# Attention 1's values and softmax sums in 32-column tiles, its padding mask by row tiles, and the segment sums in 512-column matmuls

## The chip, the cores and the metric

One NeuronCore of one Trainium2 chip runs the whole program. The metric is the device time of one execution in microseconds, the median of several runs.

## The reference

A decoder stack of four layers runs over 32 sequences of 128 tokens with 256 channels, and a context of the same shape. All arithmetic is float32.

```python
x = L0(x, ctx, Wq, Wk, Wv)          # plain attention, 16 heads; the kernel computes it for one sequence only, then adds it
# L1: Mamba-2 block, then cross attention with 8 heads of 32 channels
zxbcdt = rms(x) @ in_proj_w;  conv over 4 taps, silu
h = h * exp(dt*A) + (dt*xh) * B;  y = h . C             # a scan over the tokens, 8 heads
x = x + rms((y + D*xh) * silu(z)) @ out_proj_w
q, k, v = ln(x) @ Wq, ctx @ Wk, ctx @ Wv
scores = where(pad_mask, -1e9, q k^T / sqrt(32))
x = x + (softmax(scores) @ v) @ Wo
# L2: causal self attention and cross attention, 16 heads of 16, each + layernorm, then a small FFN + layernorm
# L3: causal cross attention, 16 heads, + layernorm, FFN with gelu
```

## The kernel before

The kernel is written engine by engine. Each sequence is a lane; four lanes (G = 4) make an iteration, and eight iterations are written out without loops. The work of a lane is cut into some 80 tasks (K1, quads1, turn1_0, values1, finish1, Wo, x2T and so on). A table of due times, `TASKS`, says when in a lane's life each task comes, in units of which 56 make an iteration and 14 the distance of one lane from the next. `in_order` sorts all tasks of the lanes in flight by due time, and every engine issues its part of each task in that one order. So in the steady part each engine's order repeats with every lane, and the order of tasks within it is that of their due times modulo 14. The first and the last iteration, in which the pipeline fills and drains, have tables of their own (`FIRST_BODY`, `LAST_BODY`). Engines run freely otherwise; semaphores make them wait.

The four attentions of a lane (a_ = 1 to 4) are units of the same steps. `quads` (L521 to L535) are the scores on TensorE: 32-row tiles side by side, each into its own bank of `score`, over a mask laid first where there is one (L521 with `ident_bf` as the full 128-row stationary operand and the padding row moving for attention 1, L526 for the causal ones). `scores` is the softmax's shift on VectorE (L1029 row maximum, L1030 subtraction, 1024 columns each) and the exponential on ScalarE (L832). `turn` transposes the exponentials on TensorE (L479, eight transposes in two halves) and ScalarE copies them to `weights` (L837). `values` are the matmuls with the values into the one bank `output`. Attention 1 has one part, the others two (`turn3_0`, `turn3_1`).

For attentions 2 to 4, `values` keeps the value block stationary in tiles of 32 columns (L572), so that channels come out on partitions; ScalarE copies `output` to `attT` (L843), TensorE turns it back (`back`), VectorE divides by the sum, which is one more column of the values (L1042, L1043, `weighted`). For attention 1, `values1` keeps the exponentials stationary (128x128) and moves the 33 columns of each head's values with a column of ones (L563), so that tokens come out on partitions. `finish1` on VectorE divides straight from `output`, `oT` turns the result on TensorE, ScalarE copies it to `actT`, and `Wo` projects it. Each use of `output` waits until the earlier user has read it (`output_read`). All other results of TensorE go through three banks, `ring`, taken in turn in the order of the tasks (`RING_JOBS`).

The Mamba block sums the log decays over segments of the sequence with triangular matrices of ones: `log_decays` on GpSimd (L1315) writes `after` times a rate into `decay`, and TensorE multiplies each of the eight heads' blocks with `before` (L641, in the task pairs).

In the trace a float32 matmul stands as two records, a bf16 matmul and a transpose as one.

Of the kernel before, what the change touches and what calls it, by code (L numbers as in the profile page):

```python
# [9 lines left out]
ALU = mybir.AluOpType  # L10
# [7 lines left out]
G = 4  # L18
# [33 lines left out]
    loadx=0.97, loadc=7.03, x1=1.35, x1r=2.07, xhat=2.42, xhatT=2.83, dt=3.57, softplus=5.74, am=7.96, xbc=3.22,  # L52
# [9 lines left out]
    finish3=37.48, norm3=37.6, x4T=37.59, fc1=38.37, fc2=38.9, norm4=39.09, K4=35.59, V4=43.75, x5T=39.37, Q4=39.68,  # L62
    xhatT=0.1, unit3=31.59, finish1=18.05, norm5=46.16, x6T=46.75, up=48.43, finish4=45.87, V3=34.69, xnT=14.02,
    proj=11.76, decayed=10.17, down=63.56, V2=23.46, softplus=5.04, am=7.89, K1=11.47, silu=8.25, pairs=9.54,
    store=74.57, quads=-0.51, K3=29.22, unit1=14.91, uT=11.66, n2=25.73, xhat=-2.92, unit4=40.55, loadc=30.78,
    dt=4.05, xbc=0.22, z=4.26, conv=7.05, Y=11.3, K2=20.29, x3T=28.9, Q2=19.77, attT=2.47, row=28.72, Q3=30.23,
    V1=9.91, Q1=14.22, x2T=19.45, loadx=-18.17, x1=-6.65, x1r=-3.34, values=3.3, norm2=28.83, oT=18.78, Wo=19.09,
    e2=21.9, unit2=21.27, n3=35.21, finish2=28.23, back=3.58, e3=35.09, turn=1.64)
LAST_BODY = dict(
    back=2.17, Q1=18.14, Q3=28.27, softplus=20.82, pairs=24.7, finish3=33.84, norm3=35.82, x4T=36.58, fc1=36.86,  # L70
    fc2=38.11, norm4=38.72, K4=37.39, V4=43.04, x5T=38.53, Q4=38.9, unit4=40.07, finish4=44.5, decayed=17.41,
    Y=-81.98, uT=31.74, proj=9.65, x1r=-32.33, values=2.12, finish2=25.14, norm2=26.85, x3T=26.95, row=27.68,
    K3=29.28, V3=26.95, e3=30.67, n3=33.63, unit3=30.43, V1=-2.63, xnT=6.1, unit1=14.68, xhatT=24.83, am=-18.19,
    down=61.44, xbc=12.12, x6T=48.84, up=52.2, Q2=19.83, V2=24.61, unit2=21.43, attT=1.73, store=41.77, turn=1.34,
    loadx=20.76, x1=-9.01, x2T=19.36, loadc=14.65, dt=-15, xhat=-2.71, z=31.47, K1=-43.07, conv=27.2, silu=-20.42,
    norm5=47.08, e2=22.59, n2=24.73, finish1=18.03, oT=17.98, Wo=18.87, K2=20.87, quads=-0.45)
# [150 lines left out]
WITHIN = """dt xnT; xbc xnT; z xnT; Q1 oT; Wo x2T; K2 x3T; Q2 x3T; V2 x3T; Q3 x4T; fc1 x5T; Q4 x6T; pairs decayed; e2 Q3; e3 Q4;  # L227
# [1202 lines left out]
```

## Time and profile before

| | |
|---|---|
| median of 3 runs | 1966.96 us (1964.62 to 1967.33) |
| the profiled execution's own time | 1966.0 us |
| its span, first to last instruction | 1964.2 us |
| TensorE matmuls, weight loads | 91%, 80% of the span |
| VectorE, ScalarE, GpSimd | 76%, 63%, 27% |
| DMA engines | busy in the first 20 us, then about 10 GB/s |
| mean granted TensorE clock | 0.97 of full speed |

The busy shares are for the whole span; the pipeline fills for some 200 us and drains for some 100. The chain of work that ended last lies on TensorE for 63% of the span and on VectorE for 28%, ScalarE has 4%.

### The profile page before, as it was taken

To read this page: it belongs to the slowest core of one execution; us is meant where nothing else is said; L and a number is where in the kernel's file an instruction comes from. 1 tells how busy PE (TensorE), PEld (TensorE's weight loads), DVE (VectorE), ACT (ScalarE), POOL (GpSimd) and SP (SyncE) were. 2 spreads that over 40 slices of the span, in tenths; PEclk is the share of its full clock that TensorE was granted. 3 is DMA by queue.
4 is the path that set the end of the run, shared out by engine and by line. 5 is a ranking of instruction groups with operands and counts; after the bars stand their busy time and mean duration, and the time that the engine had idled before them with its cause. 6 is when DMAs were issued, how large, how long until landed. Compare 5 with 4: busy or idle time off the path is not lost.

```text
span 1964.2 us, 47829 instructions
## 1 busy us (share of the span) xinstructions
PE 1796.8 (91%) x18704; PEld 1566.6 (80%) x18704; DVE 1502.0 (76%) x3163; ACT 1236.3 (63%) x2668; POOL 525.2 (27%) x1288
## 2 busy tenths in 40 slices
PE   4678899999999999999999999999999999999876
PEld 3567788888888888888888888888888888888765
DVE  3367788877888888888888888888888888788652
ACT  2245567666667766666677666667666666677443
POOL 1221323322333232223333322333232123323110
PEclk7699999999999999999999999999999999999888
DMA  6000000000000000000000000000000000000000
GB/s 231 12 4 4 2 15 4 10 10 10 10 7 10 4 10 10 10 10 10 7 4 10 10 10 10 10 7 10 5 10 10 10 10 10 7 4 4 4 4 6
DMA packets 26141, 26.46 MB, mean 13 GB/s; under 512 B 2240, under 2 KB 25024, under 8 KB 25792
## 3 DMA queue, kind: packets, MB, share of 16 engines
q1 hardware_dynamic: 25920, 23.41, 3.6%
q8 instruction: 152, 2.49, 0.5%
q14 instruction: 69, 0.57, 0.1%
HBM read 19.21 MB, written 4.19 MB: 12 GB/s over the span
## 4 chain that ended last, share of the span: by engine, by line
PE 63%; DVE 28%; issue 4%; ACT 4%; POOL 1%; DMA 0%; DVEq 0%; SPq 0%; ACTq 0%; POOLq 0%
PE ring L491 18%; PE ring L485 17%; PE ring L479 14%; DVE neg_max L1029 8%; DVE shifted L1030 7%; PE score L535 6%; PE output L563 3%; PE ring L649 3%; ACT shifted L832 2%; DVE conv L1121 1%; DVE res L1017 1%; PE score L526 1%; DVE att L1015 1%; DVE dx L1141 1%; DVE dbx L1139 1%
## 5 line engine op out<-in xcount | busy, mean ns | idle before, releaser
L1270 POOL TENSOR_TENSOR stat<-stat 128x1 f32<-128x1 f32 x224 | 125.8, 561 | 969.5 <-DVE stat L1000 961.6
L1029 DVE TENSOR_REDUCE neg_max<-score 128x8 f32<-128x1024 f32 x226 | 276.2, 1222 | 108.5 <-PE score L535 101.9
L832 ACT ACTIVATE shifted<-shifted 128x1024 f32<-128x1024 f32 x226 | 240.8, 1065 | 112.4 <-DVE shifted L1030 112.1
L1030 DVE TENSOR_TENSOR shifted<-score,neg_max 128x1024 f32<-128x1024 f32 x226 | 276.6, 1224 | 7.8
L837 ACT COPY weights<-ring 128x512 f32<-128x512 f32 x452 | 243.8, 589 | 49.3 <-PE ring L479 43.2
L479 PE MATMUL ring<-const,shifted 128*128 128x128 f32 x1808 | 249.3, 282 | 22.2 <-ACT shifted L832 19.6
L479 PEld LDWEIGHTS ring<-const,shifted 128*128 128x128 f32 x1808 | 205.2, 145 | 47.1 <-ACT shifted L832 33.4
L1113 DVE SCALAR_TENSOR_TENSOR conv<-raw,vectors,conv 128x128 f32<-128x128 f32 x576 | 184.3, 375 | 5.7
L485 PE MATMUL ring<-actT,w_q 128*128 128x128 f32 x1024 | 139.8, 281 | 4.3 <-ACT actT L809 4.3
L535 PE MATMUL score<-K,QB 32*128 32x128 f32 x3616 | 137.1, 285 | 0.3 <-ACT K L809 0.2
L485 PEld LDWEIGHTS ring<-actT,w_q 128*128 128x128 f32 x1024 | 129.9, 196 | 8.2 <-ACT actT L809 6.5
L535 PEld LDWEIGHTS score<-K,QB 32*128 32x128 f32 x3616 | 112.5, 186 | 27.3 <-issue 27.3
L809 ACT COPY actT<-ring 128x256 f32<-128x256 f32 x256 | 96.2, 377 | 53.1 <-PE ring L479 50.5
L843 ACT COPY attT<-output 128x512 f32<-128x512 f32 x97 | 56.3, 580 | 114.1 <-PE output L572 113.9
L485 PE MATMUL ring<-actT,w_up 128*128 128x128 f32 x1024 | 119.7, 275 | 0.5 <-ACT actT L809 0.5
L879 ACT ACTIVATE conv<-ring,vectors 128x128 f32<-128x128 f32 x192 | 74.6, 467 | 71.8 <-PE ring L485 71.7
L491 PE MATMUL ring<-w_down,gT 128*128 128x256 f32 x512 | 116.8, 381 | 1.3 <-issue 1.3
L485 PEld LDWEIGHTS ring<-actT,w_up 128*128 128x128 f32 x1024 | 117.2, 192 | 0.9 <-ACT actT L809 0.7
L485 PE MATMUL ring<-cT,w_k 128*128 128x128 f32 x768 | 109.9, 287 | 0.4 <-ACT raw L881 0.4
L491 PEld LDWEIGHTS ring<-w_down,gT 128*128 128x128 f32 x512 | 97.8, 192 | 14.7 <-issue 1.4
L572 PE MATMUL output<-weights,V 128*32 128x128 f32 x3104 | 105.9, 277 | 2.5 <-ACT weights L837 2.5
L491 PE MATMUL ring<-w_v,cT 128*128 128x256 f32 x384 | 101.3, 387 | 0.0
(162 smaller groups left out, 3721.6 us busy)
## 6 DMA issues: line engine op xcount, KB each, us to landing
cT<-in_ctxT SPq DMA_DIRECT2D x32, 128.0 KB, 2.1
x_in<-in_x SPq DMA_DIRECT2D x32, 128.0 KB, 2.2
out<-result SPq DMA_DIRECT2D x32, 128.0 KB, 1.7
row_all<-in_rows SPq DMA_DIRECT2D x1, 1420.0 KB, 10.4
w_in<-in_in_proj SPq DMA_DIRECT2D x1, 1288.0 KB, 7.8
w_q<-in_q SPq DMA_DIRECT2D x4, 256.0 KB, 8.3
w_k<-in_k SPq DMA_DIRECT2D x4, 256.0 KB, 6.2
w_v<-in_v SPq DMA_DIRECT2D x4, 256.0 KB, 6.7
```

What stands on the lines that cost most here:

```text
L479: last = nc.tensor.transpose(t[:, c * P:(c + 1) * P], src[:, c * P:(c + 1) * P], ident)
L485: last = mm(t[:, at:at + P], w[:, c, cols:cols + P], xT[:, c, :], start=(c == 0), stop=(c == n - 1))
L491: last = mm(t[:, at:at + hi - lo], xT[:, c, :], w[:, c, lo:hi], start=(c == 0), stop=(c == n - 1))
L535: last = mm(score[:, r, at:at + P], QB[rows_of, l, c, e, :], keys[rows_of, l, c, :], start=(not masked and at == 0), stop=(at + P == width))
L572: last = mm(output[ROWS_OF[r], four * P:(four + 1) * P], V2[:, l, h, :], exps_of(t, heads_of(a_, t).index(h)), start=True, stop=True)
L809: nc.scalar.copy(dst.rearrange("p c k -> p (c k)"), t[:, 0:n]).then_inc(read, 1)
L832: run(e, e, ACT.Exp, scale=SCALE8 if a_ == 1 else 0.25).then_inc(S["exps"], 1)
L837: nc.scalar.copy(weights[:, buffer(it, a_, l, t, WEIGHT_BUFFERS), half * 4 * P:(half + 1) * 4 * P], t_[:, :]).then_inc(read, 1)
L1029: step(nc.vector.tensor_reduce(m, s, AX_X, ALU.max, negate=True))
L1030: tt(shifted[:, n, :].rearrange("p (b h k) -> p b h k", b=shape[1], k=P), s, m.unsqueeze(3).broadcast_to(shape), ALU.add).then_inc(S["shif ...
L1113: last = stt(conv[:, l % 2, c, :], raw[:, l % 2, c, k:k + P], conv_w[:, c, k:k + 1], conv[:, l % 2, c, :], ALU.mult, ALU.add)
L1270: tt(stat[:, l, 10:11], stat[:, l, 2:3], stat[:, l, 4:5], ALU.pow).then_inc(S[done], 1)
```

## The change

- `values1`: instead of 8 matmuls with the exponentials stationary there are 16 in tiles of 32 columns with the exponentials moving: 8 with a block of ones (`ones`, 128x32) write each head's sum, repeated over its 32 channels, into the upper 256 columns of `output`, and 8 with the head's values write the products into the lower 256. `V1` has no column of ones any more.
- `finish1` on VectorE: a reciprocal of 128x256 from `output` into `rec1`, and a product of 128x256 straight into `actT`. It waits on four semaphores (one for each row tile) instead of one. The helper `weighted` serves attentions 0 and 2 to 4 alone.
- The task `oT` (two transposes, a ring job, ScalarE's copy) is gone, and `Wo` waits for `finish1`.
- `quads1`: the padding mask is laid with 32 rows of ones as the stationary operand for each row tile, the mask divided by 32.
- `pairs`: the segment sums are two matmuls with `after` stationary and 512 columns moving, instead of eight with 128; GpSimd prepares `before` times the rate instead of `after`.
- All due times differ, in the three tables.

Its core (the other due times, declarations and lists of tasks are left out):

```diff
 TASKS = dict(
...
-    z=4.31, K1=12.37, V1=13.56, conv=7.15, silu=7.78, pairs=8.82, decayed=9.65, Y=9.99, uT=10.61, proj=11.58,
-    xnT=13.12, Q1=13.77, finish1=18.09, oT=18.47, Wo=19.52, x2T=20.56, K2=20.9, Q2=20.87, V2=22.59, e2=21.84,
-    n2=25.32, finish2=27.24, norm2=28.11, x3T=29.12, row=29.4, K3=29.67, Q3=29.4, V3=32.63, e3=30.41, n3=31.69,
...
-    finish4=45.34, norm5=47.45, x6T=47.68, up=48.91, down=52.32, store=65.56, unit1=15.41, unit2=21.73, unit3=31.28,
-    unit4=39.91, quads=-0.32, scores=0, turn=1.39, values=2.22, attT=1.91, back=3.09)
...
+    z=4.22, K1=12.67, V1=14.56, conv=7.48, silu=8.18, pairs=8.71, decayed=9.11, Y=9.97, uT=10.7, proj=11.76,
+    xnT=12.98, Q1=13.57, finish1=19.59, Wo=19.69, x2T=19.74, K2=21.24, Q2=21.09, V2=22.68, e2=21.9, n2=23,
+    finish2=27.5, norm2=28.48, x3T=29.28, row=29.34, K3=29.79, Q3=29.34, V3=32.81, e3=30.68, n3=31.9, finish3=36.61,
...
+    norm5=47.41, x6T=47.95, up=49.36, down=52.34, store=56.37, unit1=15.37, unit2=21.85, unit3=31.65, unit4=39.88,
+    quads=-0.09, scores=0, turn=1.43, values=2.54, attT=1.85, back=2.97)
...
@@ -351,7 +347,9 @@
         keep = sb("keep", [P, G, H16])
         neg_max = sb("neg_max", [P, 2, HEADS])
         K1 = sb("K1", [P, G, DC, P])
-        V1 = sb("V1", [P, G, H8, DH8 + 1])
+        V1 = sb("V1", [P, G, H8, DH8])
+        ones = sb("ones", [P, DH8])
+        rec1 = sb("rec1", [P, D])
         V2 = sb("V2", [P, G, H16, P // TILES])
 
         decay = sb("decay", [P, 2, MH, P])
@@ -518,7 +516,9 @@
                     for r, rows_of in enumerate(ROWS_OF):
                         free(r)
                         if a_ == 1:
-                            mm(score[:, r, 0:width], ident_bf[:, :], padding_bf[:, :].unsqueeze(1).broadcast_to((P, DC, P)),
+
+                            mm(score[:, r, 0:width], ones_bf[rows_of, :],
+                               padding_bf[rows_of, :].unsqueeze(1).broadcast_to((P // TILES, DC, P)),
                                start=True, stop=False)
                             continue
@@ -559,10 +559,15 @@
 
                 evacuated_all(it, *V_job, *[j for t in range(PARTS[a_]) for j in turn_jobs(a_, l, t)])
                 if a_ == 1:
-                    for i, h in enumerate(heads_of(1, 0)):
-                        last = mm(output[:, h * (DH8 + 1):(h + 1) * (DH8 + 1)], exps_of(0, i), V1[:, l, h, :],
-                                  start=True, stop=True)
-                    last.then_inc(S["output_full"], 1)
+
+                    for at, summed in ((D, True), (0, False)):
+                        for c in range(DC):
+                            for r in range(TILES):
+                                h = TILES * c + r
+                                last = mm(output[ROWS_OF[r], at + c * P:at + (c + 1) * P], ones[:, :] if summed else V1[:, l, h, :],
+                                          exps_of(0, heads_of(1, 0).index(h)), start=True, stop=True)
+                                if not summed and c == DC - 1:
+                                    last.then_inc(S[f"att_full{r}"], 1)
                     return
 
                 for four in range(H16 // TILES):
@@ -637,9 +642,8 @@
                 pe.wait_ge(S["am"], nth(it, l))
                 for half in range(2):
                     t, full = claim(it, f"ld{half}", l)
-                    for i in range(4):
-                        last = mm(t[:, i * P:(i + 1) * P], decay[:, m, 4 * half + i, :], before, start=(i == 0), stop=(i == 3))
-                    last.then_inc(full, 1)
+                    mm(t[:, :], after, decay[:, m, 4 * half:4 * half + 4, :].rearrange("p h k -> p (h k)"),
+                       start=True, stop=True).then_inc(full, 1)
 
             def Y(it, l):
                 t, full = claim(it, "Y", l)
@@ -668,12 +672,8 @@
                 evacuated(it, "xnT", l, ("Q1", l))
                 project_T(it, "Q1", l, square["q1"], actT[:, l])
 
-            def oT(it, l):
+            def Wo(it, l):
                 pe.wait_ge(S["output_read"], nth_output(it, 1, l))
-                flip(it, "oT", l, att[:, l, :], DC)
-
-            def Wo(it, l):
-                evacuated(it, "oT", l, ("Wo", l))
                 project(it, "Wo", l, square["o1"], actT[:, l])
 
             def x2T(it, l):
@@ -1032,20 +1032,12 @@
 
             def weighted(it, a_, l, step, dst):
 
-                heads, dh = (H8, DH8) if a_ == 1 else (H16, DH16)
-                if a_ == 1:
-                    dve.wait_ge(S["output_full"], nth(it, l))
-                    o, read = output[:, 0:heads * (dh + 1)].rearrange("p (h e) -> p h e", h=heads), S["output_read"]
-                else:
-                    t, read = filled(it, *back_job(a_, l))
-                    o = t[:, :].rearrange("p (h e) -> p h e", h=heads)
-                step(nc.vector.reciprocal(rec[:, l, 0:heads], o[:, :, dh]))
-                tt(dst.rearrange("p (h e) -> p h e", h=heads), o[:, :, 0:dh],
-                   rec[:, l, 0:heads].unsqueeze(2).broadcast_to((P, heads, dh)), ALU.mult).then_inc(read, 1)
-                if a_ == 1:
-                    dve.wait_ge(S["output_read"], nth_output(it, a_, l))
-                else:
-                    evacuated(it, *back_job(a_, l))
+                t, read = filled(it, *back_job(a_, l))
+                o = t[:, :].rearrange("p (h e) -> p h e", h=H16)
+                step(nc.vector.reciprocal(rec[:, l, :], o[:, :, DH16]))
+                tt(dst.rearrange("p (h e) -> p h e", h=H16), o[:, :, 0:DH16],
+                   rec[:, l, :].unsqueeze(2).broadcast_to((P, H16, DH16)), ALU.mult).then_inc(read, 1)
+                evacuated(it, *back_job(a_, l))
 
             def x1(it, l):
@@ -1078,7 +1070,7 @@
             dve.wait_ge(S["rates"], 1)
             ts(decay_rate, decay_rate, -1.0, None, ALU.mult).then_inc(S["ready_in"], 1)
             ts(keep_row[:, :], pad_u8[:, :], -1.0, 1.0, ALU.mult, ALU.add)
-            ts(padding_bf[:, :], pad_u8[:, :], MASKED, None, ALU.mult)
+            ts(padding_bf[:, :], pad_u8[:, :], MASKED / (P // TILES), None, ALU.mult)
             ts(skip, skip, 0.5, None, ALU.mult)
             dve.wait_ge(S["later_in"], 16)
             ts(causal_bf[:, :, :], dx[:, 0, :].rearrange("p (q k) -> p q k", q=TILES), MASKED, None, ALU.mult)
@@ -1167,6 +1159,14 @@
                     evacuated(it, "proj", l)
                     moments(l, step, S["seed3"])
 
+                def finish1(l):
+
+                    for r in range(TILES):
+                        dve.wait_ge(S[f"att_full{r}"], nth_output(it, 1, l))
+                    step(nc.vector.reciprocal(rec1[:, :], output[:, D:]))
+                    tt(actT[:, l, :, :].rearrange("p c k -> p (c k)"), output[:, 0:D], rec1[:, :],
+                       ALU.mult).then_inc(S["output_read"], 1)
+
                 def Wo(l):
                     t, read = filled(it, "Wo", l)
                     tt(res[:, l, :], t[:, 0:D], res[:, l, :], ALU.add).then_inc(read, 1)
@@ -1261,7 +1261,7 @@
 
             nc.gpsimd.memset(V2[:, :, :, DH16 + 1:], 0.0).then_inc(S["ones_col"], 1)
             nc.gpsimd.memset(V2[:, 0, :, DH16:DH16 + 1], 1.0).then_inc(S["ones_col"], 1)
-            nc.gpsimd.memset(V1[:, :, :, DH8], 1.0).then_inc(S["ones_col"], 1)
+            nc.gpsimd.memset(ones[:, :], 1.0).then_inc(S["ones_col"], 1)
             nc.gpsimd.memset(raw[:, :, :, 0:TAPS - 1], 0.0).then_inc(S["pads_zero"], 1)
 
             def root(it, l, seed, done):
@@ -1312,7 +1312,7 @@
 
                     wait_for(S["dt"], nth(it, l))
                     step(tt(dts[:, 5, l, :], dts[:, 10, l, :], decay_rate, ALU.mult))
-                    tt(decay[:, l % 2, :, :], after.unsqueeze(1).broadcast_to((P, MH, P)),
+                    tt(decay[:, l % 2, :, :], before.unsqueeze(1).broadcast_to((P, MH, P)),
                        dts[:, 5, l, :].unsqueeze(2).broadcast_to((P, MH, P)), ALU.mult).then_inc(S["am"], 1)
 
                 def first_query(a_, l):
```

## Rows read from the trace of the kernel before

**Rows 1.** Stretches of the span: busy us of each engine, granted clock, DMA.
```profile
1000.00:1250.00 250.00, 239.48 (x2548) 209.61 (x2547) 208.47 (x440) 172.06 (x372) 77.44 (x191) 1.00 0.03 8
...
1850.00:1900.00 50.00, 39.31 (x350) 34.19 (x351) 26.18 (x53) 25.25 (x50) 5.06 (x11) 0.76 0.00 1
```

**Rows 2.** Waits of TensorE, 250 to 1750 us: total, times, longest.
```profile
PE ring L479 <- DVE att L1010: 19.9, 26, 1.1
PE ring L491 <- DVE nonzero L1180: 18.5, 26, 0.7
```

**Rows 3.** Timeline of TensorE in one period: start, us, group, records; idle in brackets.
```profile
1019.15 1.95 PE L641 MATMUL ring<-const,decay 128*128 128x128 f32 x16
...
1043.20 0.84 PE L521 MATMUL score<-padding_bf,ident_bf 128*128 128x256 bf16 x4
...
1047.76 1.08 PE L572 MATMUL output<-weights,V 128*32 128x128 f32 x32
1048.77 0.61 PE L702 MATMUL ring<-q_first,K 128*128 128x8 f32 x4
1049.45 1.09 PE L479 MATMUL ring<-const,shifted 128*128 128x128 f32 x8
1050.38 0.38 PE L479 MATMUL ring<-const,att 128*128 128x128 f32 x2
1050.69 1.17 PE L535 MATMUL score<-K,QB 32*128 32x128 f32 x32
...
1054.97 1.87 PE L563 MATMUL output<-V,weights 128*128 128x33 f32 x16
1056.68 0.17 PE L708 MATMUL ring<-nonzero,ones_bf 128*128 128x16 bf16 x1
...
1058.54 0.38 PE L479 MATMUL ring<-const,att 128*128 128x128 f32 x2
1058.76 1.03 PE L491 MATMUL ring<-w_v,cT 128*128 128x256 f32 x4
...
1062.40 1.04 PE L479 MATMUL ring<-const,shifted 128*128 128x128 f32 x8
...
1068.73 0.43 PE L526 MATMUL score<-causal_bf,ident_bf 32*32 32x512 bf16 x16
```

**Rows 4.** Timeline of ScalarE in the same period.
```profile
1060.27 1.07 ACT L837 COPY weights<-ring 128x512 f32<-128x512 f32 x2
1061.23 1.07 ACT L832 ACTIVATE shifted<-shifted 128x1024 f32<-128x1024 f32 x1
```

**Rows 5.** Timeline of VectorE in the same period.
```profile
1051.98 1.23 DVE L1029 TENSOR_REDUCE neg_max<-score 128x8 f32<-128x1024 f32 x1 [2.13 <-PE score L535]
...
1054.38 0.24 DVE L1042 RECIPROCAL rec<-ring 128x16 f32<-128x16 f32 x1
...
1056.26 0.15 DVE L1000 TENSOR_SCALAR stat<-stat 128x1 f32<-128x1 f32 x1
...
1057.30 0.42 DVE L1043 TENSOR_TENSOR att<-output,rec 128x256 f32<-128x256 f32 x1
1057.76 1.22 DVE L1029 TENSOR_REDUCE neg_max<-score 128x8 f32<-128x1024 f32 x1
1059.01 1.22 DVE L1030 TENSOR_TENSOR shifted<-score,neg_max 128x1024 f32<-128x1024 f32 x1
...
1070.38 1.22 DVE L1029 TENSOR_REDUCE neg_max<-score 128x8 f32<-128x1024 f32 x1
```

**Rows 6.** Groups by shape, whole span: count, busy us, mean ns of one, idle.
```profile
L1042 DVE RECIPROCAL rec<-ring 128x16 f32<-128x16 f32 x97 | 24.1, 248 | 27.3 <-PE ring L479 27.3
...
L1180 DVE TENSOR_SCALAR nonzero<-ring 128x16 bf16<-128x16 f32 x64 | 10.9, 170 | 23.4 <-PE ring L702 23.4
...
L1042 DVE RECIPROCAL rec<-output 128x8 f32<-128x8 f32 x32 | 6.3, 197 | 7.3 <-PE output L563 7.3
```

**Rows 7.** Line L1017 from 1000 to 1060 us: shortest, median, longest ns.
```profile
L1017 DVE SCALAR_TENSOR_TENSOR res<-att,stat,row_all x4: 484/484/873, 1003.9 to 1044.0; 128x256 f32<-128x256 f32 x4
```

More of the change, by code:

```diff
@@ L60 @@
+    finish2=27.5, norm2=28.48, x3T=29.28, row=29.34, K3=29.79, Q3=29.34, V3=32.81, e3=30.68, n3=31.9, finish3=36.61,
+    norm3=36.75, x4T=37.23, fc1=37.52, fc2=37.98, norm4=38.07, K4=36.21, V4=42.63, x5T=39.16, Q4=39.7, finish4=45.19,
+    norm5=47.41, x6T=47.95, up=49.36, down=52.34, store=56.37, unit1=15.37, unit2=21.85, unit3=31.65, unit4=39.88,
+    quads=-0.09, scores=0, turn=1.43, values=2.54, attT=1.85, back=2.97)
 FILL = (0, 14, 28, 42)
 FIRST_BODY = dict(
-    finish3=37.48, norm3=37.6, x4T=37.59, fc1=38.37, fc2=38.9, norm4=39.09, K4=35.59, V4=43.75, x5T=39.37, Q4=39.68,
@@ L63 @@
[L63 to L67, printed above, removed]
@@ L68 @@
-    e2=21.9, unit2=21.27, n3=35.21, finish2=28.23, back=3.58, e3=35.09, turn=1.64)
-LAST_BODY = dict(
[L70 to L76, printed above, removed]
+    finish3=37.33, norm3=37.37, x4T=37.59, fc1=38.04, fc2=38.55, norm4=38.92, K4=39.1, V4=43.64, x5T=39.66, Q4=39.76,
@@ new lines @@
+    xhatT=0.09, unit3=31.85, finish1=18.11, norm5=48.14, x6T=47.84, up=50.88, finish4=46.84, V3=29.86, xnT=13.05,
+    proj=11.85, decayed=10.08, down=55.89, V2=23.44, softplus=5.49, am=9.22, K1=10.91, silu=8.17, pairs=9.36,
+    store=64.14, quads=-0.41, K3=29.49, unit1=15.24, uT=11.74, n2=25.81, xhat=-0.73, unit4=41.13, loadc=33.21,
+    dt=4.25, xbc=0.34, z=4.68, conv=6.9, Y=10.24, K2=20.61, x3T=28.86, Q2=19.99, attT=2.17, row=28.82, Q3=29.22,
+    V1=7.64, Q1=14.3, x2T=19.54, loadx=-9.52, x1=-6.71, x1r=-4.39, values=2.86, norm2=28.24, Wo=19.53, e2=24.49,
@@ new lines @@
+    unit2=21.74, n3=35.42, finish2=27.88, back=3.18, e3=35.13, turn=1.78)
+LAST_BODY = dict(
+    back=1.89, Q1=19.84, Q3=29.94, softplus=32.92, pairs=-6.12, finish3=34.13, norm3=35.1, x4T=35.57, fc1=35.69,
+    fc2=36.29, norm4=37.67, K4=34.51, V4=42.78, x5T=37.53, Q4=39, unit4=40.14, finish4=44.43, decayed=14.75, Y=-71.03,
+    uT=36.09, proj=2.93, x1r=-37.16, values=1.79, finish2=26.91, norm2=28.44, x3T=29.06, row=29.64, K3=29.8, V3=34.07,
+    e3=31.51, n3=31.85, unit3=31.19, V1=-21.76, xnT=6.27, unit1=15.62, xhatT=15.25, am=-32.45, down=63.46, xbc=6.87,
+    x6T=50.06, up=53.42, Q2=21.31, V2=24.9, unit2=22.06, attT=1.75, store=34.27, turn=0.95, loadx=21.42, x1=-27.29,
+    x2T=20.17, loadc=7.04, dt=2.63, xhat=-3.03, z=20.5, K1=-29.46, conv=30.86, silu=-8.65, norm5=46.13, e2=21.99,
+    n2=24.53, finish1=17.64, Wo=19.8, K2=21.4, quads=-0.57)
@@ L223, in wait @@
         eng.wait_ge(semaphore, value)
-WITHIN = """dt xnT; xbc xnT; z xnT; Q1 oT; Wo x2T; K2 x3T; Q2 x3T; V2 x3T; Q3 x4T; fc1 x5T; Q4 x6T; pairs decayed; e2 Q3; e3 Q4;
+WITHIN = """dt xnT; xbc xnT; z xnT; xnT Q1 finish1 Wo x2T; K2 x3T; Q2 x3T; V2 x3T; Q3 x4T; fc1 x5T; Q4 x6T; pairs decayed; e2 Q3; e3 Q4;
 quads1 Q2; quads2 Q3; quads3 Q4; e2 K3 e3 K4; quads2 K3; quads3 K4; values2 V3; values3 V4; n2 e3; values2 n3; finish2 norm2;
@@ L775, in _ @@
             do = dict(K1=K_1, V1=V_1, xhatT=xhatT, xbc=xbc, z=z, pairs=pairs, Y=Y, uT=flip_u, proj=proj, xnT=xnT,
-                      Q1=Q1, oT=oT, Wo=Wo, x2T=x2T, Q2=Q2, K2=K_2, V2=V_2, x3T=x3T, row=row, Q3=Q3, K3=K3, V3=V3, x4T=x4T,
+                      Q1=Q1, Wo=Wo, x2T=x2T, Q2=Q2, K2=K_2, V2=V_2, x3T=x3T, row=row, Q3=Q3, K3=K3, V3=V3, x4T=x4T,
                       fc1=fc1, fc2=fc2, K4=K4, V4=V4,
```

13 lines of the change are left out of this document (5 added, 8 removed).

## The prediction

> **What bounds the kernel now.** I read the stretches of the span first. From about 250 to 1750 us the picture repeats: in 250 us TensorE is busy for 239.5 us at a granted clock of 1.00 (its 2.4 GHz level), VectorE for 208.5 us, and only the last hundred microseconds thin out [rows 1]. The kernel is a software pipeline with a period of one lane (one sequence). The waits of TensorE in the steady part are few and recurring: 26 waits for L1010 and 26 for L1180 in 1500 us, so the period is about 57 us, and in each TensorE stands about 0.7 us at either [rows 2]. The timeline gives the period more sharply, 56.7 us. By busy share TensorE (96%) is the bound, VectorE (83%) is not. That is too coarse, for the two hand over to each other: the softmax of a unit is two VectorE passes of 1.2 us each (L1029, L1030), then ScalarE's exponential (L832), then TensorE's transposes. So I went through one period of both engines' timelines and asked for each wait who was late. Four handovers repeat:
>
> (a) from the scores of attention 4 until the transposes of attention 1 (1049.45), VectorE works without a gap and TensorE follows it;
> (b) from there to 1062.40, the second transposes of attention 3, TensorE is the slower. VectorE waits 2.13 us for the scores of quads3, and the exponential at 1061.23 starts only when ScalarE has emptied the transposes of the first half, two copies L837 from 1060.27, though its input was ready at 1060.23 (the shift, 1059.01 + 1.22) [rows 3 to 5];
> (c) from 1062.40 until the scores of quads2 TensorE alone; VectorE reaches them at 1070.38, just as they end [rows 3, 5];
> (d) then VectorE again until x4T, and TensorE from x4T to the next quads4.
>
> **The change part by part, on TensorE.** Costs are from the start of a group to the start of the next.
>
> Values of attention 1: L563 goes, 8 matmuls (16 records) of 128x128 weights and 33 columns, 1054.97 to 1056.68, 1.71 us. In their place stand 16 matmuls in four column tiles with 128 columns moving, half of them against ones. That is the form of L572 exactly, x32 records, which takes 1047.76 to 1048.77, 1.01 us [rows 3]. Saving 0.70, less about 0.1 for changing the array's tiling, 0.6 us a lane.
>
> Padding mask: L521, four bf16 matmuls, takes 0.84 us with its tail. Four row tiles side by side should need between 0.2 (a quarter of that) and 0.43 (the causal masks in their tiles, L526) [rows 3]. So TensorE saves 0.4 to 0.65 us. It lies in stretch (a): its later two matmuls wait for the shift of attention 4 to free their score banks, and VectorE is busy there until it takes the scores. I take nothing on the path.
>
> Segment sums: L641, 8 matmuls of 128 columns, x16 in 1.95 us with the tail of the last [rows 3]; the columns stay the same (8 x 128 = 2 x 512), only six weight loads fall away. Saving 0 (columns alone count) to 0.2 us (what the group takes beyond 16 x 0.11), and x4T behind it waits for VectorE anyway: nothing. The GpSimd operation that feeds it keeps its size.
>
> oT: two transposes, 1058.54 to 1058.76, 0.22 us [rows 3], and a ScalarE copy of 128x256 with them. Their three-bank ring job goes too.
>
> Sum: 1.2 to 1.7 us of TensorE's work a lane, at most 54 us in 32 lanes if all of it counted.
>
> **On VectorE.** Before, finish1 is a reciprocal of 128x8 (197 ns) and the product (1057.30, 0.42 us) [rows 5, 6]. After, the reciprocal covers 128x256, the product stays. No row has such a reciprocal. The lower bound is what the product's own 128x256 pass costs, 0.42 us. But the two sizes that exist differ: 8 elements 197 ns, 16 elements 247 ns, while a plain operation on 16 elements is 170 ns [rows 6]. That is 50 / 8 = 6.25 ns for each further element, against (420 - 170) / 240 = 1.04 ns for the plain one. Both reciprocals lie on a line from about 150 ns. At that slope 256 elements take 247 + 240 x 6.25 = 1747 ns, and that I take: 1.75 us, 1.55 more than before. If the slope is read from rounded rows it may be a third off, so 0.42 to 2.25 us are the ends.
>
> **The new order.** All due times are changed. Sorting them for one period gives the order of every engine. Most neighbours stay; four moves matter. finish4 comes before the softmax of quads3 (scores3_0), not after, and back4 before quads3. norm5 comes before finish1. finish1 has moved from 4.09 to 5.59, after z, V3 and turn3_0 of TensorE have been issued. e2 is read before silu. n2 moves ahead of x4T and leaves two idle stretches of VectorE as they were.
>
> Stretch (b) again, with the clock of the rows: turn1_0 starts at 1049.45, back4 at 1050.38, its result is there at about 1051.0. finish4 then takes 1.96 us (before: 1054.38 to 1056.26, and 0.08 until the next could start) and lets go at 1052.96 [rows 5]; the scores of quads3 are ready at 1052.45, so they no longer make VectorE wait: 1.5 of its 2.13 us of idle time is filled. scores3_0 takes 2.40 to 1055.36, n3 0.16, norm5 0.9 (two passes; the second, L1017, takes 0.48 us in three norms of four and 0.87 in one, this one [rows 7]; if it stays slow add 0.39) to 1056.44. values1 ends on TensorE at about 1056.1 and is visible at 1056.3, so finish1 starts at 1056.45, its product at 1058.24, scores3_1 at 1058.6, and its shift ends at 1061.08. The exponential starts at 1061.11 instead of 1061.23. TensorE meanwhile is 0.83 us ahead (0.6 + 0.22): turn3_0 at 1058.8, Wo at 1059.7 without a wait for finish1, x2T at 1061.45 after VectorE's Wo, all done before 1062.28. So turn3_1 gains 0.12 us of a possible 0.83: the reciprocal eats the rest.
>
> What is queued behind the waiting instructions: on VectorE, behind finish1's four waits, scores3_1 and Wo, which are priced above; on TensorE, behind Wo's wait for the output bank, x2T, x6T and turn3_1. In (c) VectorE's convolutions end at about 1069.8, before the scores. In (a) and (d) VectorE's work is the same amount in another order, and in the second half of (d) TensorE's is too. e2 before silu ends the 0.7 us wait at L1180, but x4T, a little later, still waits for norm3 on VectorE, so the time returns as a longer wait there.
>
> Sum: 28 full periods x -0.12 = -3.4 us; in filling and draining, one unloaded lane each gains values, mask and oT with its copy (-0.6 -0.5 -0.8) and loses 1.55: -0.35, twice -0.7. In all -4.1 on the profiled execution of 1966.0 us (span 1964.2), 1962; the median of the runs is 1966.96, so 1962 to 1963. The orders written out for the first and last body also differ and could bring some 5 us either way; there the idle share is large [rows 1], and with a wait or two fewer I lean to the faster side: **1961 us**.
>
> A second rule, weighed: the Trainium skill, "TensorEngine Tiling (Array Packing)", section "Key Properties", says that a change of tiling mode drains the array. Here the group at L563 would get two such changes and the mask loses one. The rows show quads3 (a change) beginning 0.31 us after two transposes (1050.38) that elsewhere take 0.22 (1058.54) [rows 3]; at three times that price TensorE would still be ahead in (b), and the sum would stand.
>
> **The rivals.**
> Reciprocal at a plain pass's rate, or cheap otherwise (0.43 us): finish1 stops mattering, scores3_1's shift ends at 1059.76, and TensorE and ScalarE set (b). x2T then waits for VectorE's Wo until 1061.25, turn3_1 comes at about 1061.8: -0.6 a lane, -17 us, 1947. For it: nothing but that no row shows this size; against it: the slope. Chance 0.10.
> TensorE's busy time is the whole truth and VectorE yields everywhere: -1.2 to -1.5 a lane, 1921 to 1930. Against it: four handovers. Chance 0.06.
> The other side: finish1 lasts long enough that scores3_1, queued behind it, is late for the exponential. This decides from a reciprocal of 1.87 us on (1.75 + 0.12). With 2.25 us it costs 0.50 - 0.12 = 0.38 a lane, +11 us, 1977; norm5 staying slow gives the same size. By the cited page's eight cycles this would be the outcome. Chance 0.25.
> The change does its work and nothing follows: my walk is 0.1 us wrong in one stretch, which is all the gain, or the new first and last orders cost what the period brings: 1965 to 1968. Chance 0.20.
>
> **How the numbers follow.** Forecast 0.39, for 1955 to 1964. A measurement of this kernel can tell some 0.2% (4 us) from no change, so faster means under 1963, slower over 1971. Faster: most of the forecast and the two fast rivals, 0.30 + 0.10 + 0.06 = 0.46. Same: 0.09 of the forecast, 0.17 of the last rival: 0.26. Slower: 0.25 + 0.03 = 0.28. The range leaves out the 0.06 and the far ends of the bounds: 1940 to 1980.
>
> **What would show it.** L1042's successor at 128x256 near 1.75 us; L572's form in attention 1 at 1.0 us; in the period, VectorE's wait before the scores of quads3 nearly gone; the exponential of attention 3's second part starting right behind its shift; TensorE's idle time grown by over 1 us a period (longer waits at x2T and x4T), its busy share down from 96%. Wrong it would be if the reciprocal is off the line, if the period differs from 56.6 us by more than 0.3, or if the fill or drain moves by over 5 us.

## The result and the profile after

The change makes the kernel slower by a little: a median of 1976.84 us (1971.82 to 1977.95) against 1964.12 us (1961.87 to 1967.33) of the kernel before, measured beside it; ratio 1.0059 with an interval of 1.0044 to 1.0074, about 12 us. The forecast was 1961 us, faster, in a range of 1940 to 1980. The time lies in the range, but the kernel became slower and not faster. The profiled execution took 1977.95 us (span 1976.2), that of before 1966.0.

The busy times of the whole span and the stretch from 1000 to 1250 us (columns as in [rows 1]):

```profile
PE 1758.7 (89%) x18768; PEld 1487.8 (75%) x18768; DVE 1513.8 (77%) x3163; ACT 1216.9 (62%) x2636; POOL 547.4 (28%) x1288
```

```profile
1000.00:1250.00 250.00, 233.71 (x2580) 199.53 (x2571) 205.52 (x435) 167.69 (x368) 78.43 (x189) 1.00 0.03 8
```

TensorE stays at its 2.4 GHz level (1.00) and is busy for 5.8 us less in 250 us than in [rows 1]; VectorE is 3.0 us less busy, so neither engine has more to do per microsecond than before. The time went into waiting. TensorE's waits from 250 to 1750 us (total, times, longest) have a new first line, where [rows 2] had none on ScalarE:

```profile
PE ring L640 <- ACT K L945: 37.8, 26, 1.5
PE ring L477 <- DVE att L1010: 19.8, 26, 0.8
PE ring L477 <- DVE res L1017: 19.3, 52, 0.6
PE ring L477 <- DVE res L1172: 12.6, 19, 1.0
```

In every period TensorE stands 1.45 us (37.8 / 26) at L640, because ScalarE has not yet copied K4 out of the bank. L640 is the first matmul of the task `pairs`; its ring job is called CB in the code, it multiplies two blocks of the convolved channels, and the segment sums (L645) follow it. To see where the periods grew I cut each into stretches between the starts of TensorE's groups (from one `up` to the next), and took the mean over 12 to 14 periods of each kernel's timeline, which rests on many rows. In us:

| | period | up to quads2 | quads2 to CB (L640) | to x4T | to quads4 | to quads1 | to up |
|---|---|---|---|---|---|---|---|
| before | 56.73 | 3.67 | 6.39 | 3.19 | 12.74 | 8.85 | 21.88 |
| after | 57.26 | 3.67 | **6.94** | 3.19 | 12.63 | 8.94 | 21.89 |

The net growth, 0.53 us, is the 0.55 us of one stretch. The times at which VectorE writes the results (L1222) place it in the whole span: the first result comes 0.5 us earlier (247.72 us against 248.23), the second, which still belongs to the filling, 2.3 us later (294.29 against 291.95), the 27 full periods after it take 13.4 us more (until 1839.99 against 1824.19), and the draining takes 3.8 us less. That is +12.0, the difference of the two profiled executions.

These are the rows of that stretch, TensorE first. Before:

```profile
1070.20 1.08 PE L572 MATMUL output<-weights,V 128*32 128x128 f32 x32
1071.21 0.61 PE L702 MATMUL ring<-q_first,K 128*128 128x8 f32 x4
...
1073.96 1.10 PE L491 MATMUL ring<-w_v,actT 128*128 128x256 f32 x4 [0.71 <-DVE nonzero L1180]
1075.13 0.46 PE L635 MATMUL ring<-conv 128*128 128x128 f32 x2
```

After (1021.67 here is 1070.2 there):

```profile
1021.67 0.61 PE L702 MATMUL ring<-q_first,K 128*128 128x8 f32 x4
1022.21 1.08 PE L577 MATMUL output<-weights,V 128*32 128x128 f32 x32
...
1024.65 1.03 PE L489 MATMUL ring<-w_v,actT 128*128 128x256 f32 x4
1027.14 0.46 PE L640 MATMUL ring<-conv 128*128 128x128 f32 x2 [1.45 <-ACT K L945]
...
1030.33 0.44 PE L477 MATMUL ring<-const,res 128*128 128x128 f32 x2 [0.57 <-DVE res L1017]
```

values3 and e2 (L702) have changed places. In the table of due times, values3 stands at 31.28 + 2 + 2.22 = 35.50 before and at 31.65 + 2 + 2.54 = 36.19 after; modulo 14 that is 7.50 and 8.19. e2 stands at 7.84 and 7.90. The order has turned over by 0.29 of a unit. The 0.71 us wait for L1180 (`nonzero`, which reads e2) is gone, as it was to be. But in ScalarE's order the copy of values3 stands ahead of the copy of K4, whose bank CB needs. ScalarE after:

```profile
1023.52 0.58 ACT L843 COPY attT<-output 128x512 f32<-128x512 f32 x1 [1.34 <-PE output L577]
1024.13 1.28 ACT L832 ACT_TABLE_LOAD   x1
1025.42 1.06 ACT L832 ACTIVATE shifted<-shifted 128x1024 f32<-128x1024 f32 x1
1026.38 0.61 ACT L945 ACTIVATE K<-ring,vectors 128x128 f32<-128x128 f32 x2
```

ScalarE waits 1.34 us for values3, then loads the table of the exponential, then computes it, and only then copies K4 (L945). In before the same copy of values3 waits 0.29 us:

```profile
1071.51 0.58 ACT L843 COPY attT<-output 128x512 f32<-128x512 f32 x1 [0.29 <-PE output L572]
1072.12 1.28 ACT L832 ACT_TABLE_LOAD   x1
1073.41 1.06 ACT L832 ACTIVATE shifted<-shifted 128x1024 f32<-128x1024 f32 x1
1074.37 0.61 ACT L945 ACTIVATE K<-ring,vectors 128x128 f32<-128x128 f32 x2
```

From e2 or values3, whichever is first, to the copy of K4 it is 4.17 us before (1070.20 to 1074.37) and 4.71 after (1021.67 to 1026.38). The ring has three banks; CB takes the one that K4 holds. It starts late, and VectorE, which reads it at L1127, is late with it:

```profile
1027.63 0.29 DVE L1127 TENSOR_TENSOR state_gate<-ring,const 128x128 f32<-128x128 f32 x1 [0.34 <-PE ring L640]
```

norm3 (L1017) is queued behind that on VectorE, and x4T waits for it (1030.33). So the half microsecond goes from e2's place through values3, ScalarE, a ring bank and VectorE to x4T.

### The profile page after: what moved, and what is told of

It reads as the page before. It is cut to its first block, busy times and chain, and to the rows that moved or that the text cites. A ratio compares the mean times of both kernels' runs of the same rounds, so it can differ in the third digit from the quotient of the medians.

```text
span 1976.2 us, 47945 instructions
## 1 busy us (share of the span) xinstructions
PE 1758.7 (89%) x18768; PEld 1487.8 (75%) x18768; DVE 1513.8 (77%) x3163; ACT 1216.9 (62%) x2636; POOL 547.4 (28%) x1288
## 4 chain that ended last, share of the span: by engine, by line
PE 52%; DVE 32%; ACT 8%; issue 6%; POOL 1%; DMA 0%; DVEq 0%; SPq 0%; ACTq 0%; POOLq 0%
PE ring L483 16%; PE ring L477 13%; PE ring L489 10%; DVE neg_max L1029 8%; DVE shifted L1030 6%; PE score L535 4%; PE output L577 4%; ACT shifted L832 3%; PE ring L653 3%; DVE rec L1166 3%; DVE res L1017 2%; DVE att L1015 2%; ACT L832 2%; DVE bn L1004 2%; PE ring L702 2%
## 5 line engine op out<-in xcount | busy, mean ns | idle before, releaser
L1030 DVE TENSOR_TENSOR shifted<-score,neg_max 128x1024 f32<-128x1024 f32 x226 | 276.7, 1224 | 7.7
L1105 DVE SCALAR_TENSOR_TENSOR conv<-raw,vectors,conv 128x128 f32<-128x128 f32 x576 | 170.8, 351 | 5.7
L809 ACT COPY actT<-ring 128x256 f32<-128x256 f32 x224 | 79.6, 369 | 57.5 <-PE ring L477 51.9
L477 PE MATMUL ring<-const,res 128*128 128x128 f32 x320 | 63.3, 294 | 51.8 <-DVE res L1017 30.3
L1158 DVE SCALAR_TENSOR_TENSOR res<-ring,stat,res 128x256 f32<-128x256 f32 x32 | 15.5, 484 | 120.6 <-PE ring L489 120.6
```

Of the source, the lines that this page charges most:

```text
L477: last = nc.tensor.transpose(t[:, c * P:(c + 1) * P], src[:, c * P:(c + 1) * P], ident)
L809: nc.scalar.copy(dst.rearrange("p c k -> p (c k)"), t[:, 0:n]).then_inc(read, 1)
L1030: tt(shifted[:, n, :].rearrange("p (b h k) -> p b h k", b=shape[1], k=P), s, m.unsqueeze(3).broadcast_to(shape), ALU.add).then_inc(S["shif ...
L1105: last = stt(conv[:, l % 2, c, :], raw[:, l % 2, c, k:k + P], conv_w[:, c, k:k + 1], conv[:, l % 2, c, :], ALU.mult, ALU.add)
```

## The experiments

Numbers beside an experiment are its median, and the ratio to the kernel before in the same comparison with its interval. The kernel before took 1963.2 us in the first comparison (values3 back, both short reciprocals, the old order), 1964.2 in the second (the longer finish1, mask and sums, the order of my own) and 1962.6 in the third (the same swap, norm5 alone, the old first and last tables). "Mended order" means the changed kernel with values3 back ahead of e2. First the question of the period's growth. My theory after the comparison: the swap of values3 and e2. The rival: VectorE's longer reciprocal, paid for in full (1.56 us x 32 = 50 us, of which TensorE's savings give back most).

**values3 back ahead of e2**, in the changed kernel:

```
+AT["values3"] = AT["scores2_0"] + PERIOD // G + 0.02
```

> The changed kernel with one task moved: values3 on TensorE stands before e2 again, as it did in the kernel before (its due time in the steady table is set just behind scores2_0; first and last body as they are). Theory 1 (ScalarE's order sets the lost half microsecond): values3 ends 0.54 us earlier in each period, so ScalarE's copy to attT, the table load behind it, the exponential of scores2_0 and the copy-out of K4 come 0.5 us earlier, the CB matmul of pairs no longer makes VectorE's L1127 wait, and the period falls from 57.19 to about 56.75 us: 1977 - 13 = 1964 us (1961 to 1967). Theory 2 (the long reciprocal itself is the loss, VectorE is simply fuller): no change, 1975 to 1979 us.

Measured 1960.16 us, 0.9986 (0.9976 to 0.9996), a little under the range named. Period 56.71, and quads2 to CB 6.39 again, all other stretches as in after. The swap accounts for the whole growth of the period. TensorE still waits for K4:

```profile
PE ring L641 <- ACT K L946: 24.2, 26, 0.9
```

but its 0.9 us a period costs nothing, since VectorE comes to its reader of CB (L1128) at 1017.13, 0.62 us after CB starts (1016.51), without waiting.

**The same swap alone in the kernel before**:

```
+AT["values3"] = AT["e2"] + PERIOD // G + 0.01
```

> The kernel before with one task moved and nothing of the change: values3 on TensorE stands behind e2 instead of before it, the neighbourhood that the change made. Theory 1: this alone costs what the changed kernel lost; ScalarE's copy to attT, table load, exponential of scores2_0 and K4's copy-out come 0.5 us later, CB waits for them, and the period grows by 0.4 to 0.5 us: 1964 + 13 = 1977 us (1973 to 1979). Rival (the loss needs the long reciprocal or the other moves beside it): 1962 to 1967 us.

Measured 1985.37 us, 1.0116 (1.0100 to 1.0132): 23 us slower, period 57.59, quads2 to CB 7.26. The sign and the place are as expected with neither the long reciprocal nor any new matmul; the size is larger. The timeline of TensorE shows why:

```profile
1024.14 0.58 PE L703 MATMUL ring<-q_first,K 128*128 128x8 f32 x4 [0.23 <-POOL q_first L1323]
1024.65 1.08 PE L573 MATMUL output<-weights,V 128*32 128x128 f32 x32
...
1029.58 0.46 PE L636 MATMUL ring<-conv 128*128 128x128 f32 x2 [0.87 <-ACT K L946]
```

e2 needs an input of GpSimd (`q_first`) that in the old order is ready just too late, 0.23 us here and 0.29 in the mean of 26 waits, so values3 starts that much later still: 0.55 + 0.29 is close to the 0.87 us by which the stretch grew.

**A short reciprocal**, with and without the order mended; it divides only by 16 of the 256 columns:

```
-step(nc.vector.reciprocal(rec1[:, :], output[:, D:]))
+step(nc.vector.reciprocal(rec1[:, 0:16], output[:, D:D + 16]))
```

> The changed kernel with the reciprocal of finish1 cut to 16 of its 256 columns (the other 240 factors are constant ones, so that part of the softmax's division is left out); everything else, the order too, as changed. Theory 1: the reciprocal is worth only what TensorE and ScalarE are ahead in the stretch before turn3_1: 0.5 to 0.7 us of the 1.5 us saved reach the path, 1977 - 17 = 1960 us (1957 to 1964). Theory 2: VectorE's work counts in full, 32 x 1.5 = 48 us, 1929 us.

Measured 1966.15 us, 1.0011 (1.0000 to 1.0023). That is outside the range named. 0.45 us a period goes in the stretch to `up` (21.89 to 21.44), as expected, but quads2 to CB grows from 6.94 to 7.10: quads2 now comes earlier and GpSimd's `q_first` doesn't. GpSimd is done with it at 1014.75, and e2 starts at 1014.90, 1.64 us after quads2 instead of 1.47. So e2's place costs more here too. With values3 ahead of e2 as well:

> Both edits: values3 before e2, and the reciprocal over 16 of 256 columns (the division is left out for the other 240). Theory 1: the two losses lie in different stretches of the period and add: 1977 - 13 - 17 = 1947 us (1943 to 1951). Theory 2: what the short reciprocal alone gives, no more.

Measured 1947.11 us, 0.9916 (0.9899 to 0.9933): 0.45 us a period against the mended order alone, nothing elsewhere (period 56.25). 1.5 us less on VectorE is worth 0.45: the rest is covered by TensorE and ScalarE, as stretch (b) of the prediction had it. The rival, VectorE's time in full, falls. The prediction's rival with a cheap reciprocal gave 1947 as well; it holds with the order mended, not in the changed kernel's own order (1966).

**A longer finish1**: an extra reciprocal of 128 columns ahead of the real one, order mended:

```
+step(nc.vector.reciprocal(rec1[:, 0:P], output[:, D:D + P]))
```

> a_values3 with a second reciprocal over 128 of the columns ahead of the first (same results, 0.15 + 128 x 0.00625 + step = about 1.0 us more on VectorE). Theory 1: at 1.75 us the reciprocal is already what the exponential of scores3_1 waits for, so every further microsecond counts in full: +1.0 us a lane, 1960 + 28 = 1988 us (1984 to 1993), while taking 1.5 us away gave only 0.46. Rival (VectorE has slack left there): less than half of it, under 1975 us.

Measured 2001.38 us, 1.0187 (1.0170 to 1.0204): 41 us above the mended order, 1.38 us a period in the stretch to `up` for an operation of 0.96 us (957 ns by its group's mean; start to start about 1.00). TensorE's wait for Wo's sum (L1174) grows to 1.6 us at a time:

```profile
PE ring L478 <- DVE res L1174: 30.2, 19, 1.6
```

That more than the operation's own time is lost was not expected. The periods one by one show why. An ordinary one takes 57.65 us, 1.0 more than with the mended order (56.65), so on this side of the balance the operation counts in full, once. But four of the 26 periods between 250 and 1750 us, and one more behind them, take about 59.3. In these the matmuls that follow the 1.6 us wait are slow, and so is the granted clock. First an ordinary period, then a long one, rows of TensorE and the stretch in question:

```profile
848.63 1.09 PE L478 MATMUL ring<-const,shifted 128*128 128x128 f32 x8
849.55 1.06 PE L484 MATMUL ring<-actT,w_q 128*128 128x128 f32 x8
848.60:851.60 3.00, 2.97 (x27) 2.98 (x28) 2.18 (x9) 2.58 (x8) 2.01 (x7) 1.00 0.03 5
```

```profile
906.28 1.75 PE L478 MATMUL ring<-const,shifted 128*128 128x128 f32 x8
907.83 1.91 PE L484 MATMUL ring<-actT,w_q 128*128 128x128 f32 x8
906.20:909.50 3.30, 3.22 (x16) 3.22 (x17) 2.41 (x9) 1.84 (x6) 2.22 (x8) 0.55 0.02 5
```

For some 3 us TensorE stands near its 1.2 GHz level (0.55), which costs 1.65 us each time. The groups of eight on `w_q` never take over 1.2 us between 250 and 1800 us in before, after or the mended order; in the latter two the longest wait at this place is 1.0 us. Why only some of the 1.6 us waits have this effect is not shown.

**The old order with the new operations** (the three old tables of due times, without oT):

> The changed code in the old order: all three tables of due times are those of the kernel before, without oT. Theory 1, walked through the rows of before with the 1.75 us reciprocal: scores3_1 is shifted by 1061.05 as now, but norm5, Wo and x2T now come after it, so turn3_1 starts some 0.3 us later than in the kernel before, and nothing is gained elsewhere: 1964 + 9 = 1973 us (1968 to 1980). Theory 2 (the new order costs the half microsecond and the code would pay with the old one): TensorE's saving shows, 1925 to 1950 us.

Measured 1967.48 us, 1.0018 (1.0007 to 1.0028), just below the range named. The period is 57.07: +0.34 us, 0.09 in the stretch to quads1 and 0.25 in the next, where a walk as for stretch (b) gives 0.3. So in the old order the long reciprocal costs about what its rows say, and the new order is what hides it, but for its misplaced values3. 27 x 0.34 would be 9 us, 4.3 were measured: the other 5 are won while the pipeline fills and drains (first result at 243.86 us against 248.23).

**Mask and segment sums alone in the kernel before** (the values, the order and oT stay):

```
-mm(score[:, r, 0:width], ident_bf[:, :], padding_bf...broadcast_to((P, DC, P)),
+mm(score[:, r, 0:width], ones_bf[rows_of, :], padding_bf[rows_of, :]...broadcast_to((P // TILES, DC, P)),
-for i in range(4): last = mm(t[:, i * P:(i + 1) * P], decay[:, m, 4 * half + i, :], before, ...)
+mm(t[:, :], after, decay[:, m, 4 * half:4 * half + 4, :].rearrange("p h k -> p (h k)"), ...)
```

> The kernel before with two parts of the change alone: the padding mask by row tiles and the segment sums in 512-column matmuls (GpSimd writes before times the rate). Order, values1, finish1 and oT as before. Theory 1 (both lie where TensorE waits for VectorE anyway): no change, 1960 to 1966 us beside 1963, period 56.7. Rival (TensorE's busy time sets the end): about 0.45 us a lane, 14 us less, 1949 us.

Measured 1959.03 us, 0.9973 (0.9964 to 0.9982), with a period of 56.73, that of before. In the steady part the two edits are worth nothing, as the prediction said, yet 5 us are won, 1 more than the range named allows. They lie outside it: in the profiled executions the first result comes at 246.06 us against 248.23, and from the last steady result to the last of all it is 131 us against 137. **The counterpart**, mended order with mask and sums as before:

> a_values3 with these two parts taken back, so that of the change only the values, sums, finish1, the lost oT and the order are left. Theory 1: no change against a_values3, 1958 to 1963 us. Rival: 14 us more, 1974 us.

Measured 1964.62 us, 1.0003 (0.9994 to 1.0013), 4.5 us above the mended order at the same period (56.73). That is outside its range (1958 to 1963), and the two comparisons agree: some 5 us in filling and draining. How they come about there is not settled. The clock has a part in it: from 1850 us to the end the mean granted clock is 0.89 with the new mask and sums and 0.82 in before, which by the two levels is about 23 us at 1.2 GHz against 41. And the time of any of these kernels goes with its mean granted clock: in this comparison the kernel before took 1963.1 us in its 8 executions at 0.976 and 1967.3 in its 2 at 0.971. At 0.976 the mask and sums took 1960.3 us (3 executions), so 2.8 of the 5.2 us stand at an equal clock. Whether the rest is the edits' doing, by a drain that lets the clock stay up, or the other way round is open.

**An order of my own** for norm5, n3 and values1, which was to bring the gain that the reciprocal ate:

```
+AT["n3"], AT["values1"] = AT["quads3"] + 0.01, AT["quads3"] - PERIOD // G + 0.02
+AT["norm5"], AT["x6T"] = AT["scores3_1"] + PERIOD // G + 0.02, AT["Wo"] + 2 * (PERIOD // G) + 0.02
```

> a_values3 with four more tasks moved in the steady table: n3 and values1 before xbc, norm5 behind scores3_1, x6T between Wo and x2T. Then finish1 no longer waits for norm5's 0.95 us nor for xbc on TensorE. Theory 1: the exponential of scores3_1 comes 0.95 us earlier, of which 0.5 to 0.57 us reach turn3_1 (x2T then waits for Wo on VectorE): period 56.2 us, 1960 - 15 = 1945 us (1942 to 1952). Rival: another wait takes its place (x6T for norm5, or the exponential of scores3_0, now behind a later xbc on ScalarE): 1956 to 1965 us.

Measured 1987.17 us, 1.0114 (1.0094 to 1.0133): wrong by 42 us. The convolutions of VectorE now run beside GpSimd's gating (two operations of 1.51 and 1.28 us), and the silu product behind them beside its 1.90 us decay product, and both stretch. In after the gating is over before the convolutions begin. The first two rows are of after, the others of this kernel:

```profile
1013.88 1.27 POOL L1309 TENSOR_TENSOR zs<-tz,zs 128x512 f32<-128x512 f32 x1
1015.79 5.44 DVE L1105 SCALAR_TENSOR_TENSOR conv<-raw,vectors,conv 128x128 f32<-128x128 f32 x18
```

```profile
1019.93 1.28 POOL L1312 TENSOR_TENSOR zs<-tz,zs 128x512 f32<-128x512 f32 x1
1019.42 6.84 DVE L1108 SCALAR_TENSOR_TENSOR conv<-raw,vectors,conv 128x128 f32<-128x128 f32 x18
...
1028.65 1.54 DVE L1116 SCALAR_TENSOR_TENSOR conv<-raw,conv 128x768 f32<-128x768 f32 x1
```

By stretches 0.66 us a period is lost between CB and x4T (3.85 instead of 3.19), where norm3 stands behind the longer silu product on VectorE, and 0.20 in the stretch to `up` (22.08).

**norm5 alone** (the second line):

> Half of av_norm5: a_values3 with norm5 behind scores3_1 and x6T between Wo and x2T, while n3 and values1 stay behind xbc. If av_norm5 lost its time through the later xbc (a later exponential of scores3_0, and GpSimd's gating running beside VectorE's convolutions), this one is near a_values3 or 0.1 to 0.2 us a lane better: 1955 to 1962 us. If norm5's new place was the loss, 1975 us or more.

Measured 1974.76 us, 1.0060 (1.0045 to 1.0076), at the edge of what norm5's place as the loss was to give. norm5's new place costs 0.49 us a period in the stretch to `up`, and transposes of norm results now wait for VectorE three times a period:

```profile
PE ring L479 <- DVE res L1019: 54.0, 78, 1.3
```

So norm5's place alone costs 15 us, and n3 and values1 on top of it bring the loss to 27. The two parts don't simply add: with all four moves the stretch to `up` loses only 0.20 us, and the 0.66 us before x4T appear only then (3.19 with norm5 alone).

**The mended order with the old first and last tables**:

> a_values3 with the first and last tables of the kernel before (without oT); the steady order is a_values3's. The first result came 1 to 2 us earlier with the old first table (a_oldorder 243.9 us, a_values3 244.8 us), the drains took 134.5 and 134.2 us. So 1 to 3 us less than a_values3: 1958 us (1956 to 1961).

Measured 1958.81 us, 0.9983 (0.9971 to 0.9995). It beats the kernel before and the changed one, but not mask and sums alone (1959.03, in the second comparison): the values and the new order add nothing measurable to them.

## Why the prediction was wrong, point by point

**Confirmed: the reciprocal.** Predicted 1.75 us from the slope of [rows 6] (with the row's 248 ns for the 247 written there it is 1.78), measured

```profile
L1166 DVE RECIPROCAL rec<-output 128x256 f32<-128x256 f32 x32 | 56.2, 1756 | 7.0 <-PE output L567 6.6 <-issue 0.4
```

Two sizes in the trace were enough to price a third sixteen times as large. By the Trainium skill, "VectorE: DVE Perf Modes", section "Walkthrough: the 8-slice pipeline in each mode" (a repeat count of 8), it would have been the estimate of 2.25 us; the measurement decides for 1.756.

**Confirmed: TensorE's operations.** From start to start, values 1.01 us (1006.72 to 1007.73; 1.71 before, so 0.70 saved with nothing to see of the 0.1 taken off for the tiling), mask 0.37 (994.69 to 995.06; bounds 0.2 and 0.43), both halves of the segment sums 1.72 (1027.87 to 1029.59); with its tail that group is 0.07 us shorter than before (1.88 against 1.95):

```profile
994.69 0.65 PE L520 MATMUL score<-padding_bf,ones_bf 32*128 32x256 bf16 x4
995.06 0.73 PE L535 MATMUL score<-K,QB 32*128 32x128 f32 x16
...
1006.72 0.64 PE L567 MATMUL output<-weights,ones 128*32 128x128 f32 x16
1007.18 0.62 PE L567 MATMUL output<-weights,V 128*32 128x128 f32 x16
1007.73 2.02 PE L489 MATMUL ring<-w_in,actT 128*128 128x264 f32 x8
...
1027.87 1.88 PE L645 MATMUL ring<-decay,const 128*128 128x512 f32 x4
1029.59 0.17 PE L708 MATMUL ring<-nonzero,ones_bf 128*128 128x16 bf16 x1
```

**Confirmed: stretch (b), row by row.** 48.48 us are to be added to compare with [rows 4, 5] (turn1_0 starts at 1000.97 here):

```profile
1002.53 0.26 DVE L1037 RECIPROCAL rec<-ring 128x16 f32<-128x16 f32 x1 [1.04 <-PE ring L477]
...
1004.53 1.22 DVE L1029 TENSOR_REDUCE neg_max<-score 128x8 f32<-128x1024 f32 x1
...
1007.58 0.48 DVE L1017 SCALAR_TENSOR_TENSOR res<-att,stat,row_all 128x256 f32<-128x256 f32 x1
1008.07 1.76 DVE L1166 RECIPROCAL rec<-output 128x256 f32<-128x256 f32 x1
1009.86 0.42 DVE L1167 TENSOR_TENSOR actT<-output,rec 128x256 f32<-128x256 f32 x1
1010.20 1.21 DVE L1029 TENSOR_REDUCE neg_max<-score 128x8 f32<-128x1024 f32 x1
```

finish4 at 1051.01 (predicted 1051.0), the maxima of quads3 at 1053.01 without a wait (1052.96), the reciprocal at 1056.55 (1056.45), the product at 1058.34 (1058.24), scores3_1 at 1058.68 (1058.6). norm5's slow pass (0.87 us, [rows 7]) has become a fast one (0.48); the prediction counted on that, and had it stayed slow, 0.39 us more would have been due. From turn1_0 to turn3_1 it is 12.85 us in most periods, 12.96 before: turn3_1 gains 0.11 us, 0.12 were predicted.

**The step that failed: "In (a) and (d) VectorE's work is the same amount in another order, and in the second half of (d) TensorE's is too."** I counted the amounts of work and stopped there. The order within (d) decides too: "e2 before silu ends the 0.7 us wait at L1180, but x4T, a little later, still waits for norm3 on VectorE, so the time returns as a longer wait there" followed the edit on VectorE only. e2 is read before silu because e2 is computed earlier, and on TensorE that puts values3 behind it. Neither the step of 0.29 units in the sorted due times nor the chain values3, copy, table load, exponential, copy of K4, bank was walked; I had listed four moves as those that matter, and this one is not among them. It costs 0.55 us a period (the two orders of the changed kernel differ by that alone), where the whole term for (d) was zero.

**The slower rival was right in its number for another reason.** It gave 1977 us, and 1976.84 came, but through a reciprocal of over 1.87 us or norm5 staying slow. Neither happened: 1.756 us, and 0.48. So its number was met by luck. Its mechanism does exist, as the extra reciprocal shows: past the balance, more time in finish1 counts in full.

**The term for (b), -0.12 us a period, was right there but not in the sum.** With the order mended, the period is 56.71 against 56.73. To quads4 0.11 us is won, to quads1 0.09 lost, and the last stretch is unchanged. The boundary at quads1 means little: with the old mask that stretch is 8.85 and the next 21.97, and the new mask alone in the kernel before gives 8.93 and 21.80, so the shorter mask only moves a boundary within work that VectorE sets. Counted from quads4, turn1_0 comes 0.11 us later. On VectorE the way from norm2 (L1015) to the shift of scores1_0 (L1030) has grown from 3.58 to 3.67 us; all that has changed in these rows is that x1 stands ahead of V4 and the token mask's three operations instead of behind them. Then (b) wins its 0.11. From turn3_1 to `up` it is 0.05 more, and two of 14 periods take 0.3 us longer at Wo's sum, 0.04 in the mean. So the term of zero for (a) was wrong too, by 0.1 us, again through an order that was not walked, and it cancels the gain of (b). That x1's place is the cause was not tested by itself.

**Filling and draining: the term of -0.7 for both together was too small in size.** In the profiled executions the second result comes 2.3 us later and the drain is 3.8 us shorter, and the mask with the sums alone is worth 5 us there. This fits a reading in which TensorE's shorter work counts where the lanes are few, but only the size is shown, not the path, and part of it goes with the granted clock. The forecast's 28 full periods are 27 by the stored results.

**The signs named in advance.** VectorE's wait before quads3's scores is gone and TensorE idles more, both as stated; the period is 57.26, 0.66 us from the 56.6 promised, which was the sign for "wrong", and the table by stretches led from it to the place.

## What to carry to other kernels

When due times change, sort them for every engine and write down each pair of neighbours that has turned over, also where both are cheap: here a swap of two TensorE groups of 0.5 and 1 us cost 15 us, more than all the arithmetic of the change was worth. Follow each swapped group through whoever copies it out of its buffer, and what stands behind that copy on the same engine. A saving on an engine that is already waiting is worth nothing in the steady part, and may still be worth a few microseconds where the pipeline fills and drains.

## What the runs showed of the hardware

- A reciprocal costs 6.3 ns an element in a row against about 1.0 for a product of the same shape: 128x8, 128x16, 128x128 and 128x256 took 197, 248, 957 and 1756 ns ([rows 6] and above).
- ScalarE, which alternates between two sets of functions here, loads the exponential's table in 1.28 us, and the exponential starts 0.01 us behind the load (1024.13 + 1.28, 1025.42). The Trainium skill, "ScalarE: Activation LUTs", section "What ACT_TABLE_LOAD costs", has the same 1283 ns and a drain of 1380 ns beside it; these rows show no such gap ahead of the load (0.03 us after the copy) or behind it.
- VectorE's operations on SBUF stretch when GpSimd runs long ones beside them: the same 18 convolutions took 5.44 us in the changed kernel, where GpSimd's gating ends before them, 5.97 in the kernel before, where a GpSimd operation of 0.72 us overlaps their start, and 6.84 with norm5, n3 and values1 moved, where the gating runs beside them; the silu product of 128x768 took 0.95 us and, beside the decay product, 1.54.
- A wait can cost TensorE more than its own length. With the longer finish1 it waits 1.6 us at one place in every period, and in one period of five or six the granted clock is 0.55 for the 3.3 us behind it: eight transposes took 1.75 us instead of 1.09, the projection behind them (x8 records) 1.91 instead of 1.06. No such group is slow in the steady part of the kernels before and after.
